# A decoder layer on one core: a second value tile, one staging tile for energies and heads, and all five instruction lists written anew

## The chip, the cores and the metric

The kernel runs on one core of a Trainium2 chip. The metric is the device time of one execution in microseconds (us); lower is better. Engines are called as in the profile: PE (TensorE, matmuls), DVE (VectorE), ACT (ScalarE), POOL (GpSimd), and SP (SyncE), which here issues nearly all DMAs.

## The reference

Four batches of 512 tokens with 512 channels go through one layer of three blocks. Each block adds its result to its input and normalises each row.

```python
Q, K, V = (X @ W.T + b for each of Wq, Wk, Wv)          # 16 heads of 32; Q, K scaled by 32 ** -0.25
scores  = where(causal, Q @ K.T, -inf)
x = layernorm(x + softmax(scores) @ V @ Wo.T + bo)
q, k    = ctx @ Wq.T + bq, ctx @ Wk.T + bk              # 512 x 128, from a context of 256 channels
x = layernorm(x + x @ softmax(q @ k.T).T)               # over the 512 x 512 energies of the batch
xq = quantise(rms_norm(x))                              # 8-bit steps with a scale for each row
x = layernorm(x + ((silu(xq @ sign(Wg).T) * (xq @ sign(Wu).T)) @ sign(Wd).T))    # hidden 2048
```

## The kernel before

A step s is one half batch of 256 tokens (two tiles t of 128); batch b has steps 2b and 2b+1, and a label such as `op1.0.1` means batch 1, half 0, tile 1. For precision most operands are held as two 16-bit parts, a high part that ACT writes and a low part (the rest) that POOL or DVE writes, and PE multiplies high by high, low by high and high by low.

The work of a step, by the names in the lists:

- `lw`, `lg`, `lx`, `lc`, `lr`, `bi`, `sm` (SP): loads of weights, of the 12 pieces of 1 MB whose signs the feed-forward block uses, of x, of the context, of rows, of biases. `ws`, `sg`, `xs`, `cs` split them or take their signs; `kb` (POOL) scales the biases, which the first `qk` on ACT waits for.
- `qk`, `va`: projections on PE; ACT and DVE write both parts of queries and keys (tile `qk`) and of values (tile `v`, with a column of ones, set once by a memset).
- `sk` (SP): three DMAs that copy the parts of one head (of four) of a pair of head groups into the tile `st`, where the score matmuls read them. `mx`: scores for the row maxima, reduced by DVE; `nm`: these maxima transposed; `sh` (SP): two DMAs that put them into `st` as a row, so that `st` (PE) computes scores less the maximum.
- `st`, `sx`, `hi`, `lo`: exponentials on ACT, a causal mask on POOL, high and low parts. `pv` (PE): weights by values; `ov`: division by the row sum.
- `to`: the heads' output is split into the staging tile `ohl` (ACT, POOL) and turned by a transposing DMA (SP) for `op`, the output projection. `os` and `tx` (the same kind of turn, tile `rhl`) lead to `xm`, the cross product.
- `cp`, `en`, `ez`, `ta`: the context's projections, the energies of a batch in four tiles, their softmax, their split into the staging tile `ehl` and their turn by DMA into `aT`, which `xm` reads.
- `n1`, `n2`, `tq`, `ib`, `ga`/`gg`, `uu`, `hw`, `hd`, `hh`, `dn`, `zn`: quantisation and the feed-forward block in 8 units, the last norm and the store.

What sets the order of the work is five lists written into the file, one for each engine (`SP_ORDER`, `PE_ORDER`, `ACT_ORDER`, `DVE_ORDER`, `POOL_ORDER`). Each engine takes its list strictly in order; a step whose inputs are not there holds up all that follows in its list. In PE's list the number behind @ is the PSUM bank (of 8) that the step uses; a bank is opened again when the engine that empties it is done.

`v` holds one batch, so ACT's copy of the first values of a batch waits until the last `pv` of the batch before has read it: `wait(act, pv_done, s // 2 * 2, 0)`. `ohl` has one slot for each tile of a step, `ehl` two slots for the four energy tiles: a slot is written again when the turn that read it has landed.

## Time and profile before

| what | value |
|---|---|
| median of 3 runs (lowest to highest) | 622.56 us (620.17 to 625.86) |
| profiled execution, time / span | 619.0 us / 617.3 us |
| busy in the span: PE, DVE, ACT, POOL | 583.5, 487.6, 413.0, 395.0 us |
| mean granted clock of TensorE | 0.987 |
| DMA: q1, issued by SP | 58.89 MB, 36.4% of 16 engines' span |

The span goes from the first to the last instruction of the profiled execution; its time holds 1.7 us more around it. A busy PE is the union of its matmuls. In the rows further down, a bracket with an arrow says how long an engine was idle before an instruction and what ended that; "SPq" is SP's queue, whose duration is that of issuing, not that of the transfer. L635 issues the stacks, L646 the energies' turns, L600 the sign pieces, L1122 reduces the maxima.

### The profile page before, as it was taken

Reading aid. Unit: us, or ns where it says so; the run is one execution under the profiler, and the core shown is the slowest. Engines: PE = TensorE matmul, PEld = TensorE weight load, DVE = VectorE, ACT = ScalarE, POOL = GpSimd, SP = SyncE. Lnnn points to the kernel's source line nnn. Section 1 sums busy time; section 2 is a strip of 40 time slices with the busy share of each in tenths; the row PEclk is TensorE's granted clock in tenths of the full one; section 3 lists DMA queues with packets and bytes.
Section 4 is the critical chain, followed back from the end, with each engine's and each line's share of the span. In section 5 each row is a group of like instructions: output and inputs, shape, how many; then the busy total and the mean of one; then the engine's idle time right before and its main releaser. Section 6 shows DMA issues by size and latency. Waiting matters only on the chain.

```text
span 617.3 us, 13871 instructions
## 1 busy us (share of the span) xinstructions
PE 583.5 (95%) x5100; PEld 389.1 (63%) x5100; DVE 487.6 (79%) x1296; ACT 413.0 (67%) x773; POOL 395.0 (64%) x518
## 2 busy tenths in 40 slices
...
GB/s 302 323 206 230 253 174 53 129 256 86 10 47 105 91 70 37 49 158 91 78 39 46 146 69 19 3 103 120 36 51 53 105 87 36 10 90 56 19 35 34
DMA packets 90851, 60.29 MB, mean 98 GB/s; under 512 B 65056, under 2 KB 81952, under 8 KB 89248
## 3 DMA queue, kind: packets, MB, share of 16 engines
q1 hardware_dynamic: 90240, 58.89, 36.4%
...
## 4 chain that ended last, share of the span: by engine, by line
PE 66%; SPq 11%; DMA 6%; DVE 6%; ACT 6%; issue 3%; POOL 2%; ACTq 0%; POOLq 0%; DVEq 0%
PE ps_b L700 24%; PE ps_b L851 16%; PE ps_b L866 14%; SPq L635 9%; PE ps_b L795 4%; PE ps_b L774 4%; PE ps_b L757 2%; DMA st<-qk 2%; PE ps_b L753 1%; DMA oT<-ohl 1%; DMA bx<-in_b_x_dram 1%; DVE ps_b L1122 1%; ACT ps_b L961 1%; ACT p L947 1%; ACT ph L884 1%
## 5 line engine op out<-in xcount | busy, mean ns | idle before, releaser
L1122 DVE CUSTOM_DVE_ANT_0 ps_b<-ps_b,future 128x256 f32<-128x256 f32 (+3 forms) x256 | 118.7, 517 | 16.9 <-PE ps_b L757 10.4
L1317 POOL TENSOR_TENSOR ph<-p,ph 128x512 f16<-128x512 f32 x96 | 110.0, 1161 | 27.2 <-ACT ph L884 26.5
L851 PE MATMUL ps_b<-xqT,sg 128*128 128x256 f16 x1024 | 124.9, 272 | 0.1
L866 PE MATMUL ps_b<-sd,hp 128*128 128x512 fp8e4 x512 | 119.1, 379 | 0.0
L1313 POOL TENSOR_TENSOR hp<-gt,hp 128x512 f16<-128x512 f32 x64 | 74.0, 1161 | 56.6 <-ACT hp L884 56.2
L851 PEld LDWEIGHTS ps_b<-xqT,sg 128*128 128x128 fp8e4 x1024 | 98.0, 98 | 19.0 <-ACT p L947 0.6
L700 PE MATMUL ps_b<-xhl,wh 128*128 128x256 f16 x480 | 84.8, 275 | 1.4 <-DVE wl L1073 1.3
L866 PEld LDWEIGHTS ps_b<-sd,hp 128*128 128x128 f16 x512 | 48.6, 98 | 50.0 <-POOL hp L1313 1.5
L1274 POOL TENSOR_SCALAR_AFFINE_SELECT p<-p 128x256 f32<-128x256 f32 (+1 forms) x96 | 46.5, 494 | 46.2 <-ACT p L947 45.7
L700 PE MATMUL ps_b<-xhl,wl 128*128 128x256 f16 x240 | 66.0, 275 | 0.0
L947 ACT ACTIVATE p<-ps_b 128x512 f32<-128x512 f32 x96 | 54.1, 594 | 16.8 <-PE ps_b L774 16.5
L884 ACT ACTIVATE ph<-p 128x512 f16<-128x512 f32 x96 | 58.0, 634 | 9.3 <-POOL p L1274 9.0
L884 ACT ACTIVATE hp<-gt 128x512 f16<-128x512 f32 x64 | 39.9, 628 | 30.8 <-DVE gt L1239 28.1
L1060 DVE TENSOR_TENSOR ph<-ps_b,ph 128x512 f16<-128x512 f32 x64 | 43.2, 685 | 20.9 <-ACT ps_b L961 20.9
L774 PE MATMUL ps_b<-st 128*128 128x256 f16 (+1 forms) x384 | 53.9, 260 | 1.7 <-DVE tops L1122 1.2
L1032 ACT ACTIVATE gt<-gt 128x512 f32<-128x512 f32 x64 | 40.1, 626 | 19.5 <-DVE gt L1226 18.9
L700 PEld LDWEIGHTS ps_b<-xhl,wh 128*128 128x128 f16 x480 | 47.3, 99 | 9.1 <-DVE wl L1073 1.9
L1231 DVE SCALAR_TENSOR_TENSOR gt<-gt,ps_b 128x512 f32<-128x512 f32 x64 | 43.6, 682 | 11.6 <-ACT gt L1032 11.0
L1226 DVE TENSOR_TENSOR gt<-ps_b,invb 128x512 f32<-128x512 f32 x64 | 43.6, 686 | 9.6 <-POOL hp L1313 5.9
L795 PEld LDWEIGHTS ps_b<-v,ph 128*128 128x128 f16 x1376 | 46.4, 97 | 6.4 <-DVE tops L1122 1.2
L795 PE MATMUL ps_b<-v,ph 128*128 128x65 f16 (+2 forms) x1376 | 48.5, 184 | 0.5 <-DVE ph L1060 0.3
L1239 DVE SCALAR_TENSOR_TENSOR gt<-gt,ps_b 128x512 f32<-128x512 f32 x64 | 43.1, 682 | 5.4 <-PE ps_b L851 4.5
...
## 6 DMA issues: line engine op xcount, KB each, us to landing
...
```

Of the source, the lines that this page charges most:

```text
L635: sp.dma_start(st[DH * r:DH * (r + 1), q:k + 1:k - q, j, :, :], qk[DH * j:DH * (j + 1), gp, first:first + step + 1:step, :, :])\
L700: ins = pe.matmul(ps, lhs(hl, c), rhs(hr, c), start=n == 0, stop=n == len(todo) - 1)
L774: ins = pe.matmul(ps[:, col:col + HALF - first], st[:, Q_SLOTS + 2 * gp + kt // 2, j, g % 2, kt % 2 * P:(kt % 2 + 1) * P], st[:, (2 * s + ...
L795: ins = pe.matmul(ps[:, col:col + width], ph[:, n % PH_SLOTS, half, at:at + P], v[:, kt, HG * g + j, first:first + width], start=kt == hal ...
L851: ins = pe.matmul(ps[:, a * HALF:(a + 1) * HALF], sg[:, ("gg", "uu").index(name), c, ht * P:(ht + 1) * P], xqT[:, c, :], start=c == 0, sto ...
L866: ins = pe.matmul(ps[:, :], hp[:, (UNITS * s + n) % HP_SLOTS, h, a, t * P:(t + 1) * P], sd[:, ht, :], start=ht == h == 0, stop=ht == HT - ...
L884: act.activation(out_, in_, ACT.Copy, scale=scale).then_inc(signal, 1)
L947: act.activation(p32[:, m % P32_SLOTS, :], ps[:, :], ACT.Exp, scale=EXP_SCALE).then_inc(p_exp.sem, 1)
L1122: ins = dve.tensor_tensor_reduce(scores, scores, future[:, S - width:S], 1.0, -3e38, ALU.add, ALU.max, tops[:, g // 2, j:j + 1, g % 2, qt ...
L1274: pool.affine_select(out=blocks, in_=blocks, pattern=[[0, len(cols)], [1, P]], compare_op=ALU.is_ge, fill=0.0, base=0, channel_multiplier= ...
L1313: pool.tensor_tensor(slot[:, 1, :, :], tg[:, n % 2, :, :], slot[:, 0, :, :], ALU.subtract)\
L1317: pool.tensor_tensor(out_, in_, hi, ALU.subtract).then_inc(signal, 1)
```

## The change

The value tile has two copies; batch b uses copy b mod 2, and ACT's copy of values waits for the weighing of the batch before the last one. The staging tile `ehl` is gone: energies are split into `ohl`, in the slot t mod 2. So that neither overwrites the other, energies wait until the heads of the batch before are turned, and heads until the energies of their own batch are turned. The scratch for dynamic DMAs falls from 4096 to 1024. All five lists are new: the same steps in another order (about one word in six stands at its old place), and PE's banks are dealt out anew. Of the lists the beginnings of SP's and ACT's are shown; further down the new ACT list has `sg9` and `sg10` right behind `va1.0.0`, where the old one has `sg8` and `sg9` right ahead of it.

```diff
 SP_ORDER = """
-lw0.0 lw0.1 lw0.3 lw0.2 lw2.0 lw1.1 lw1.3 lw2.1 lw1.0 sm lw1.2 lx1 lw2.2 lw3 bi lw2.3 lc0 lg0 lg1 lr0 lr1 sk0.0.0.2
-sk0.0.0.0 sk0.0.0.1 sk0.0.1.3 sk0.0.0.3 sk0.0.1.2 lg2 sk0.0.1.1 lg3 sk0.0.1.0 lx2 lg4 sk0.1.0.0 sh0.0.0 sk0.1.0.2
-sk0.1.0.3 sk0.1.0.1 lg5 lg6 ta0.0 ta0.1 sh0.0.1 lg7 lx3 sk0.1.1.2 sk0.1.1.0 sk0.1.1.1 sh0.1.0 sk0.1.1.3 lg8 ta0.2 lg9
-sh0.1.1 sk1.0.0.1 sk1.0.0.0 sk1.0.0.2 to0.0.0 to0.0.1 sk1.0.0.3 tx0.0.0 lc1 ta0.3 sk1.0.1.0 sk1.0.1.2 tx0.0.1 lg11
+lw1.1 lw1.2 lw0.0 lw1.3 lw0.1 lw1.0 lw2.1 bi lw0.2 lw0.3 lw2.2 lc0 lx1 lw2.0 lw3 lw2.3 sm lg0 lg1 lr1 lr0 sk0.0.0.1
+lg2 sk0.0.0.2 sk0.0.1.3 sk0.0.0.0 sk0.0.0.3 lx2 lg3 sk0.0.1.1 sk0.0.1.0 lg4 ta0.0 sk0.0.1.2 ta0.1 lg5 sk0.1.0.0
+sh0.0.0 sk0.1.0.3 sk0.1.0.1 sk0.1.0.2 lg6 ta0.2 lg7 ta0.3 sh0.0.1 lc1 lg8 sk0.1.1.0 sk0.1.1.1 sk0.1.1.3 sk0.1.1.2
+sh0.1.0 lg9 lx3 lg10 sh0.1.1 to0.0.0 sk1.0.0.1 to0.0.1 sk1.0.0.0 sk1.0.0.3 sk1.0.0.2 tx0.0.0 sk1.0.1.0 tx0.0.1
...
 ACT_ORDER = """
-lx0 xs0.0.0 ws0.0 xs0.0.1 ws0.1 ws0.2 ws0.3 ws1.0 ws1.1 bv ws1.2 ws1.3 ws2.0 ws2.1 ws2.2 wx qk0.0.0 ws2.3 ws3 cs0.0
-qk0.0.1 cs0.1 sg0 qk0.0.2 qk0.0.3 va0.0.0 sg1 cp0.0 cp0.1 va0.0.1 xs0.1.0 xs0.1.1 en0.0 qk0.1.0 sg2 qk0.1.1 ez0.0
-en0.1 nm0.0.0 ta0.0 ez0.1 sg3 en0.2 qk0.1.2 va0.1.0 ez0.2 ta0.1 sg4 st0.0.0.0 qk0.1.3 hi0.0.0.0 st0.0.0.1 va0.1.1
...
-nm0.1.1 to0.0.1 st0.1.1.4 sx0.1.1.3 sx0.1.1.5 sx0.1.1.6 qk1.0.2 st0.1.2.0 st0.1.2.1 ov0.1.0 sx0.1.2.2 hi0.1.1.1
-hi0.1.1.4 en0.3 hi0.1.2.0 ez0.3 st0.1.2.4 st0.1.3.0 qk1.0.3 st0.1.3.1 ov0.1.1 hi0.1.2.1 hi0.1.2.4 sx0.1.2.3 st0.1.3.4
-sx0.1.2.5 sx0.1.2.6 sx0.1.3.2 tx0.0.0 ta0.3 hi0.1.3.0 hi0.1.3.1 sx0.1.3.3 sx0.1.3.5 sx0.1.3.6 hi0.1.3.4 ov0.1.2
-tx0.0.1 sg8 sg9 va1.0.0 ov0.1.3 va1.0.1 to0.1.0 to0.1.1 nm1.0.0 xs1.1.0 xs1.1.1 n10.0.0 n10.0.1 sg10 sg11 ib0
+lx0 xs0.0.0 xs0.0.1 ws0.0 ws0.1 ws0.2 ws0.3 ws1.0 ws1.1 ws1.2 ws1.3 cs0.0 cs0.1 ws2.0 ws2.1 ws2.2 qk0.0.0 ws2.3 ws3 bv
+qk0.0.1 qk0.0.2 sg0 wx qk0.0.3 sg1 va0.0.0 va0.0.1 cp0.0 cp0.1 xs0.1.0 xs0.1.1 sg2 en0.0 en0.1 ez0.0 ez0.1 ta0.0 ta0.1
+qk0.1.0 en0.2 sg3 ez0.2 qk0.1.1 nm0.0.0 sg4 qk0.1.2 en0.3 ta0.2 ez0.3 ta0.3 sg5 va0.1.0 va0.1.1 st0.0.0.0 st0.0.0.1
+hi0.0.0.0 hi0.0.0.1 qk0.1.3 nm0.0.1 st0.0.0.2 st0.0.1.0 st0.0.1.1 hi0.0.0.2 hi0.0.1.0 xs1.0.0 xs1.0.1 sg6 ov0.0.0
...
 POOL_ORDER = """
-k0 k1 kb cs0.0 cs0.1 xs0.1.0 xs0.1.1 rb0.0.0 rb0.0.1 rb0.1.0 rb0.1.1 ta0.0 ta0.1 st0.0.0.0 lo0.0.0.0 st0.0.0.1
+k0 k1 cs0.0 cs0.1 kb xs0.1.0 xs0.1.1 rb0.0.0 rb0.0.1 rb0.1.0 rb0.1.1 ta0.0 ta0.1 ta0.2 ta0.3 st0.0.0.0 st0.0.0.1
...
-        v = sb("v", [P, T, NH, VW], F16)
+        v = sb("v", [P, 2, T, NH, VW], F16)
...
-        ehl = sb("ehl", [P, 2, 2, S], F16)
...
             def turn_energies(b, t):
                 wait(sp, ta_lo, b, t + 1)
                 wait(sp, x2_sum, 2 * b, 0)
-                turn(aT, t, ehl[:, t % 2, :, :], ta_in[t % 2])
+                turn(aT, t, ohl[:, t % 2, :, :], ta_in[t % 2])
...
-                                            v[:, kt, HG * g + j, first:first + width],
+                                            v[:, s // 2 % 2, kt, HG * g + j, first:first + width],
...
             def values(s, t):
-                wait_for(act, vconsts, 1)
+                wait_for(act, vconsts, 2)
                 act.wait_ge(*filled("va", s, t))
                 ps = bank_of("va", s, t)
-                wait(act, pv_done, s // 2 * 2, 0)
-                split(v[:, 2 * (s % 2) + t, :, 0:DH], ps[:, :].rearrange("p (h d) -> p h d", h=NH), v_hi.sem, 1 / WSCALE)
+                wait(act, pv_done, s // 2 * 2 - 2, 0)
+                split(v[:, s // 2 % 2, 2 * (s % 2) + t, :, 0:DH], ps[:, :].rearrange("p (h d) -> p h d", h=NH), v_hi.sem, 1 / WSCALE)
...
             def flip_energies(b, t):
                 wait(act, e_norm, b, t + 1)
                 wait(act, ta_in[t % 2], b, t // 2 * 16)
-                split(ehl[:, t % 2, 0, :], e32[:, t % 2, :], ta_hi.sem)
+                wait(act, to_in[t % 2], 2 * b, 0)
+                split(ohl[:, t % 2, 0, :], e32[:, t % 2, :], ta_hi.sem)
 
             def flip_heads(s, t):
                 wait(act, o_out, s, NG)
                 wait(act, to_in[t], s, 0)
+                wait(act, ta_in[t], s // 2, T // 2 * 16)
                 split(ohl[:, t, 0, :].rearrange("p (g d) -> p g d", g=NG), o[:, s % 2, :, t, :], to_hi.sem)
...
-                dve.memset(v[:, :, :, DH:DH + 1], 1.0).then_inc(vconsts, 1)
+                for i in range(2):
+                    dve.memset(v[:, i, :, :, DH:DH + 1], 1.0).then_inc(vconsts, 1)
...
-    nc = bacc.Bacc("TRN2", target_bir_lowering=False, num_devices=1, dynamic_dma_scratch_size=4096)
+    nc = bacc.Bacc("TRN2", target_bir_lowering=False, num_devices=1, dynamic_dma_scratch_size=1024)
```

## Rows read from the trace of the kernel before

**Rows 1.** The stretches: busy us (x instructions) of PE, PEld, DVE, ACT, POOL; PEclk; DMA; GB/s.

```profile
0.00:26.00 26.00, 14.96 (x102) 10.76 (x103) 13.97 (x24) 15.90 (x28) 16.88 (x17) 1.00 0.90 324
...
58.00:96.00 38.00, 31.17 (x329) 20.42 (x328) 29.04 (x90) 32.98 (x62) 30.28 (x37) 0.82 0.72 198
96.00:132.00 36.00, 33.52 (x369) 21.44 (x367) 26.41 (x82) 31.64 (x61) 22.49 (x32) 1.00 0.61 139
132.00:600.00 468.00, 463.19 (x4047) 312.16 (x4046) 386.57 (x996) 305.76 (x581) 306.33 (x414) 1.00 0.28 68
...
611.40:617.30 5.90, 0.00 (x0) 0.00 (x0) 2.55 (x5) 0.00 (x0) 2.48 (x6) 0.80 0.24 89
```

**Rows 2.** PE's waits, whole span: us in total, times, longest.

```profile
PE ps_b L757 <- DMA st<-qk: 5.3, 5, 2.1
```

**Rows 3.** SP's queue in order of time, 57 to 82 us: start, us, form, xcount.

```profile
57.84 0.58 SPq L600 DMA_DIRECT2D gt<-in_sgT_dram  x1
...
58.97 7.34 SPq L646 DMA_TRANSPOSE aT<-ehl  x2
...
70.71 5.82 SPq L635 DMA_DIRECT2D st<-qk  x9
...
80.47 1.31 SPq L646 DMA_TRANSPOSE aT<-ehl  x1
```

**Rows 4.** DVE in order of time, 74 to 97 us; in brackets the idle time before.

```profile
79.83 0.70 DVE L1122 CUSTOM_DVE_ANT_0 ps_b<-ps_b,future 128x512 f32<-128x512 f32 x1 [5.21 <-PE ps_b L753]
...
85.25 0.43 DVE L1143 TENSOR_TENSOR ps_b<-ps_b,o 128x224 f32<-128x224 f32 x1
...
85.88 0.42 DVE L1148 TENSOR_TENSOR o<-ps_b,osum 128x256 f32<-128x256 f32 x1
...
95.61 0.27 DVE L1129 SCALAR_TENSOR_TENSOR mrow<-ps_b,mrow 16x128 f16<-16x128 f32 x1
```

**Rows 5.** ACT in order of time, 120 to 127 us.

```profile
122.98 0.60 ACT L884 ACTIVATE v<-ps_b 128x512 f16<-128x512 f32 x1
```

**Rows 6.** SP's queue, 340 to 354 us.

```profile
343.89 1.25 SPq L646 DMA_TRANSPOSE aT<-ehl  x1
```

**Rows 7.** DMA issues by form: median us from issue to landing at the end.

```profile
aT<-ehl SPq DMA_TRANSPOSE x16, 3.2
```

**Rows 8.** ACT in order of time, 346 to 352 us.

```profile
349.85 1.14 ACT L884 ACTIVATE ohl<-o 128x512 f16<-128x512 f32 x2
```

**Rows 9.** PE in order of time, 20 to 24 us.

```profile
22.80 0.61 PE L700 MATMUL ps_b<-wh,xhl 128*128 128x512 f16 x2 [3.15 <-DVE wl L1073]
```

**Rows 10.** ACT in order of time, 17 to 22 us.

```profile
20.39 0.84 ACT L926 ACTIVATE qk<-ps_b,bqk 128x256 f16<-128x256 f32 x2 [2.65 <-POOL bx L1375]
```

**Rows 11.** POOL in order of time, 15 to 24 us.

```profile
19.49 0.28 POOL L1374 TENSOR_SCALAR bqk<-bqk 128x8 f32<-128x8 f32 x1 [3.95 <-DMA bx<-in_b_x_dram]
```

**Rows 12.** SP's waits, 26 to 82 us: us in total, times, longest.

```profile
SPq L635 <- DVE qk L1104: 1.5, 1, 1.5
SPq L600 <- ACT sg L911: 1.1, 1, 1.1
```

**Rows 13.** ACT in order of time, 30 to 58 us.

```profile
49.41 1.90 ACT L911 ACTIVATE sg<-gt 128x2048 fp8e4<-128x2048 f32 x1
...
53.84 0.62 ACT L884 ACTIVATE ehl<-e 128x512 f16<-128x512 f32 x1
```

**Rows 14.** SP's queue, 90 to 131 us.

```profile
99.20 5.80 SPq L635 DMA_DIRECT2D st<-qk  x9
105.11 3.34 SPq L646 DMA_TRANSPOSE oT<-ohl  x2
```

**Rows 15.** PE's waits, 96 to 132 us.

```profile
PE ps_b L700 <- DMA oT<-ohl: 1.2, 1, 1.2
```

**Rows 16.** Other stretches, for the granted clock (PEclk).

```profile
79.00:89.30 10.30, 9.32 (x89) 5.83 (x87) 9.22 (x28) 7.46 (x13) 5.63 (x8) 0.50 0.82 249
89.30:96.00 6.70, 5.15 (x80) 3.01 (x79) 6.30 (x19) 6.70 (x15) 5.76 (x7) 1.00 0.02 5
```

More of the change, by code:

```diff
@@ L248 @@
+zn3.0.1 ga3.1.1 hh3.1.0 hh3.1.1 ga3.1.2 ga3.1.3 hh3.1.2 hh3.1.3 ga3.1.4 ga3.1.5 hh3.1.4 hh3.1.5 ga3.1.6 ga3.1.7
+hh3.1.6 hh3.1.7
 """
 DVE_ORDER = """
-k0 xs0.0.0 ws0.0 xs0.0.1 ws0.1 ws0.2 ws0.3 ws1.0 ws1.1 ws1.2 ws1.3 wx ws2.0 ws2.1 ws2.2 bv qk0.0.0 ws2.3 ws3 qk0.0.1
-qk0.0.2 qk0.0.3 va0.0.0 cp0.0 cp0.1 va0.0.1 bo mx0.0.0.0 mx0.0.0.1 en0.0 mx0.0.0.2 mx0.0.1.0 mx0.0.1.1 mx0.0.1.2 en0.1
-en0.2 ez0.0 qk0.1.0 qk0.1.1 ez0.1 nm0.0.0 mx0.0.2.0 mx0.0.2.1 mx0.0.2.2 ez0.2 mx0.0.3.0 mx0.0.3.1 va0.1.0 mx0.0.3.2
```

427 lines of the change are left out of this document (216 added, 211 removed).

## The prediction

> **What bounds the kernel now.** Read the stretches first [rows 1]: what counts is where TensorE (PE) stands idle, since its matmuls are the same before and after. From 132 to 600 us it is busy for 463.19 of 468 us: 4.8 us to win there. The tail after its last matmul is 5.9 us. The rest of the idle time lies in the head: 11.0 us before 26 us (weights arrive), then 6.8 us of the 38 us from 58 to 96, and 2.5 us from 96 to 132. In the head another engine sets the pace. The list of PE's waits [rows 2] shows stacks (st<-qk, the copies that put queries and keys where the score matmuls read them) as a main cause. Their issues stand in SP's queue [rows 3]: from the sign load at 57.84 to the stacks at 70.71 it waits next to nothing, and the first stack of the second pair of head groups goes out only at 70.71. VectorE (DVE) idles 5.21 us for it until 79.83 [rows 4] and then works without a break to 95.88, 16 us, on row maxima that all later steps need. From there ScalarE (ACT) is the busiest after PE, 31.64 of 36 us [rows 1]. So a new order can win in the head, a little in the middle, and nothing in the tail, where the last down products come in the same way.
>
> **The second value tile.** It lets ACT copy the values of batch b before the weighing of batch b-1 has ended. In the shown execution that copy for batch 1 runs at 122.98 with no idle time of ACT ahead of it [rows 5]: the engine was late, not the tile. PE takes its list in order and is 99% busy from there on, so an earlier start only moves work: nothing gained, and the bound is the 4.8 us of idle time after 132 us [rows 1]. The second memset of ones is some 0.1 us on an idle DVE: nothing. The readers of v only address another tile in turn; no operation changes in size. The scratch falls from 4 KB to 1 KB; the DMAs here are issued by SP and ACT, so I count nothing.
>
> **The shared staging tile.** Two waits are new. Energies of batch b wait until the heads of batch b-1 are turned; these lie far apart. Heads of batch b wait until all four energy tiles of that batch are turned. In batch 2 the last of those turns is issued from 343.89 for 1.25 us [rows 6], an energy turn lands 3.2 us after its issue [rows 7], so by about 348.3, and ACT takes the heads at 349.85 [rows 8]. The wait is covered by 1.5 us. If the cover went, the exponentials and tanh steps behind it on ACT would wait as long: 0 to +2 us for a batch, taken as 0. In batch 0 the old order could not stand: it took the heads first and the fourth energy tile later. That is why en0.3, ez0.3 and ta0.3 move far ahead on four engines.
>
> **The start, 0 to 26 us.** Weight chunks of K now come first, those of Q later. By the issue order the first matmul starts some 1.5 us later. But the next hard stop is the value projection at 22.80, which waited 3.15 us for the last V chunk [rows 9]. Its low part stands on DVE behind the first query step, which on ACT stood behind POOL's bias scaling [rows 10, 11]: it waited 2.65 us for it. In the new order POOL scales the bias behind two context steps, so this stop stays near 20.4 us on ACT, although bias and K come sooner. PE has one projection more behind it by then and stalls for the context weights instead. Sum: 0, between -1.5 and +1.5 us.
>
> **The head, 26 to 96 us.** SP is the queue to follow. Ahead of the second pair's stacks of step 1 it issued 12.9 us of other things (two sign loads, two energy turns, a shift row, a sign load, x). The new order puts there again three sign loads, two turns (ta0.2, ta0.3), the shift row and a context load: the same to within 1 us. But lg5, ta0.0 and ta0.1, which stood there, now come still earlier, ahead of the first pair's stacks. A sign load takes 0.58 us, a turn 1.31 us when free (80.47), and both turns together 7.34 us when two loads of 1 MB were ahead of them [rows 3]. So SP gets 3.2 to 7.9 us more to do, less the 1.5 and 1.1 us that it waited there before [rows 12]: +0.6 to +5.3 us. The new list asks for the stacks of head 0 first, which is worth one stack, -1 to -2 us. DVE's 16 us chain takes in one more divide (like that from 85.25 to 86.30, 1.05 us), a transposed row of maxima (0.27) and a query step of two operations (by the one of 0.42, some 0.9): +2.2 us [rows 4]. Sum: +0.8 (0.6 - 2 + 2.2) to +6.5 us (5.3 - 1 + 2.2). A single load stands directly ahead of each turn now, as at 80.47, so I take the lower part: +3.
>
> **The head, 96 to 132 us.** Here the new order gives back. On ACT the list from the second shift row to the first value copy of batch 1 loses two sign pieces at 1.90 us and five smaller ones (en0.3, ez0.3, ta0.3, an exponential, a high part) at about 0.62 [rows 13]: 6.9 us less, since they were done earlier or (one sign piece) are done later. On SP the turn to0.0.0 was issued at 105.11, behind nine stack DMAs of 5.80 us [rows 14], and PE waited 1.2 us for it [rows 15]; it now stands ahead of them. PE can get back no more than its idle time: 2.5 us here and 1.5 us from 89.3 to 96 [rows 1, 16]. Sum: -1 to -5, taken -3.5 as ACT has over 6 us of room.
>
> A rule of the Trainium skill speaks against my counting of the queue. DMA: Bandwidth & Descriptors, section Issuing engines are not separate DMA queues, says that the time in which a sequencer starts DMAs is usually small beside the DMA itself. Here nine stack DMAs keep SP for 5.82 us [rows 3], 0.65 us each, and their order sets when DVE may go on; the trace disagrees. By that rule SP's part (+0.6 to +5.3) would be nothing and the sum some 2 us lower.
>
> **After 132 us.** All lists are new. Counted in steps of PE's list from 132 us on, the new one is as tight as the old: between a transposed maximum and the first score that needs it lie at least 2 steps (before 3), between project_out and its cross at least 7 (before 6). The bound is -3 (of 4.8 us of idle time) to +5 us, taken 0. Tail: 0.
>
> **Sum.** 0 + 3 - 3.5 + 0 = -0.5 us against the profiled execution's 619.0 us (span 617.3): 618.5. The median of the three runs, 622.56, lies 3.6 us above that execution, so I expect 622 us as a median. A measurement of this kernel can tell about 1% (6.2 us) from no change, so this is no change.
>
> **Rivals.** First, slower: SP's queue becomes the bound. Place: ta0.1 and ta0.3, each behind a 1 MB load that has not drained. Price: the pair that took 7.34 us less two free turns of 1.31, so 4.7 us for each of the two [rows 3]; the head is then +3 + 9.4 - 3.5 = +9 and the time 631. It decides from the point where two turns need over 4 us of issue each. For it speaks that four turns now share that queue with seven sign loads; against it the free turn at 80.47. Chance 0.18.
>
> Second, faster: the turns are free, DVE's 5.21 us gap closes because head 0 is asked for first, ACT's relief is paid out in full. Then -1 from 26 to 96, -5 from 96 to 132, -2 later: -8, time 614. For it speaks that DVE idled there; against it that the stacks come no earlier in SP's order. Chance 0.24.
>
> Third, the clock. The granted clock was 0.50 from 79.0 to 89.3, just after PE had stood waiting for stacks, and 1.00 afterwards [rows 16]. It cost little, as DVE was the bound. If a longer stall puts such a stretch where PE is the bound (after 96), it costs half of 10.3 us, +5: 627. Chance 0.05. The Trainium skill, TensorE: Matmul & The Clock Gate, section HAM oscillation — how this bites in real kernels, says that waits on DMAs can put the array back to its slow clock; the row agrees.
>
> That the change does not do what it says (the value tile never in the way) is in the forecast, chance 0.53, whose own range is 616 to 628.
>
> **How the numbers follow.** Faster by over 1% is most of the second rival and a little of the forecast's low end: 0.24. Slower by over 1% is most of the first rival and some of the forecast's and the clock's high ends: 0.18. The rest, 0.58, is no change. The range goes to both rivals: 613 to 631.
>
> **What would show it.** Right: PE idle from 58 to 96 us at 6 to 10 us and from 96 to 132 under 2 us; PE still over 98% busy from 132 to 600; sk0.1.1.0 issued between 70 and 76 us; DVE's chain of maxima ending at 97 to 101; value copies that are ready before the last weighing without PE gaining. Wrong: two energy turns of over 4 us each on SP (slower); that chain ending before 95 (faster); a stretch at half clock after 96; ACT idle for several us ahead of a heads copy, or over 10 us of PE idle after 132, which would be the shared tile or the new lists in the middle.

## The result, and the profile of the changed kernel

The changed kernel took **625.49 us** (median of 17 runs, 623.42 to 629.01), the kernel before in the same rounds 620.33 us (618.63 to 626.59): a ratio of **1.0065 (1.0044 to 1.0086)**, some 4 us slower where half a microsecond less was forecast. Repeated in other rounds it gave 1.0098 (1.0066 to 1.013). So the loss is 4 to 6 us; it is smaller than the 1% bound of the forecast, and larger than its own interval. The profiled execution took 627.9 us (span 626.2), 8.9 us more than that of before; part of this is scatter, since it lies 2.4 us above its median and that of before 1.3 us below its own.

The stretches of the changed kernel, with the columns of [rows 1]:

```profile
0.00:26.00 26.00, 16.88 (x115) 12.33 (x116) 15.14 (x23) 16.25 (x29) 18.10 (x18) 1.00 0.88 324
26.00:58.00 32.00, 24.70 (x160) 15.30 (x158) 18.46 (x67) 21.40 (x35) 9.42 (x8) 0.95 0.97 234
58.00:96.00 38.00, 30.60 (x288) 20.36 (x288) 28.93 (x107) 32.90 (x59) 26.13 (x33) 0.87 0.73 234
96.00:132.00 36.00, 33.14 (x417) 22.45 (x417) 27.85 (x85) 33.81 (x67) 22.62 (x29) 1.00 0.41 90
132.00:600.00 468.00, 458.95 (x4003) 308.70 (x4002) 388.88 (x994) 302.29 (x576) 308.34 (x420) 1.00 0.31 68
...
72.00:82.00 10.00, 7.37 (x43) 5.30 (x43) 4.77 (x17) 7.45 (x12) 6.80 (x10) 0.54 0.91 285
...
364.00:377.00 13.00, 9.67 (x87) 5.19 (x86) 7.89 (x16) 5.27 (x11) 6.32 (x8) 0.87 0.52 81
371.00:376.00 5.00, 4.79 (x18) 2.02 (x19) 1.73 (x5) 0.41 (x2) 1.34 (x2) 0.66 0.28 52
```

Beside [rows 1], PE idles 9.1 instead of 11.0 us in the first 26 us, 7.3 from 26 to 58, 7.4 instead of 6.8 from 58 to 96, 2.9 instead of 2.5 from 96 to 132, and 9.1 instead of 4.8 after that. From 26 to 58 us the kernel before had this row, so 2.6 us of idle time:

```profile
26.00:58.00 32.00, 29.37 (x209) 19.27 (x208) 22.13 (x94) 23.15 (x39) 11.89 (x11) 1.00 0.72 220
```

Two places stand out: 26 to 58 us, and 364 to 377 us, where PE is idle for 3.3 us and a half clock begins. PE's waits over the whole span, beside [rows 2]:

```profile
PE ps_b L757 <- DMA st<-qk: 9.0, 7, 3.8
...
PE ps_b L774 <- DMA st<-mrow: 3.3, 2, 2.6
...
PE ps_b L700 <- DMA x1T<-rhl: 1.9, 1, 1.9
```

Idle time alone misses the half clock. So I use **lost time** below: PE's list holds the same matmuls in every kernel, and each step has a duration when nothing waits and the clock is full (2.59 us for a projection, 0.22 for a score, some 564 for all; an estimate from the steps that nothing held up). The start of a step, less these durations of all steps ahead of it in the list, is the time lost until then. Taken from the profiled execution of each kernel, in stretches of that work (the first 100 us end about where the first scores of batch 1 stand; the third is the stretch around the first cross product of batch 2, `xm2.0.0`):

```
lost us up to ...      100   320   340   end   sum
before                37.0   6.9   0.2   3.2  47.4
changed               41.6   4.9   4.9   4.9  56.3
changed, repeated     41.4   5.6   4.2   4.2  55.4
tiles_old_lists       36.6   8.2   0.2   3.7  48.8
new_head_old_rest     40.2  10.6   0.2   3.4  54.5
old_head_new_rest     37.6   7.5   2.9   3.9  52.0
old_head_new_rest_2   38.2   9.9   4.8   3.9  56.8
signs_after_stacks    42.6   5.1   2.8   4.7  55.2
signs_and_act         41.1   5.3   4.7   4.3  55.4
signs_act_chain       43.8   5.5   4.6   4.6  58.5
early_shift           38.1   5.2   4.5   5.1  53.0
early_shift_signs     40.6   5.1   4.4   4.6  54.7
sg8_back              40.4  13.4   2.7   4.5  61.1
second_shift_early    46.0   5.4   2.8   4.3  58.6
before_stacks_first   42.9   8.9   0.2   3.0  55.0
cross_later           40.0   5.3   6.5   3.7  55.6
rows_early            41.9   5.2   0.7   4.3  52.1
first_shift_rows      42.8   5.2   0.7   4.9  53.6
both_shifts_rows      46.6   4.4   0.7   4.1  55.8
before_rows_late      38.1   8.7   1.7   4.0  52.5
```

The head costs some 4 us more, the cross of batch 2 another 4 to 5, and between them the new lists lose less than the old. One profile stands behind each line, so a difference of a microsecond or two says little: the unedited new head alone lies between 40.0 and 41.9 in five profiles, and its last exponential of batch 0 ends between 120.8 and 123.0 us.

**The head.** SP's queue of the changed kernel from 47 to 85 us, with the columns of [rows 3]:

```profile
47.21 4.69 SPq L635 DMA_DIRECT2D st<-qk  x3
51.95 2.42 SPq L646 DMA_TRANSPOSE aT<-ohl  x1
...
64.70 1.28 SPq L646 DMA_TRANSPOSE aT<-ohl  x1
66.02 0.58 SPq L600 DMA_DIRECT2D gt<-in_sgT_dram  x1
66.64 3.15 SPq L646 DMA_TRANSPOSE aT<-ohl  x1
69.83 1.23 SPq L643 DMA_DIRECT2D st<-mrow  x2
...
73.83 7.83 SPq L635 DMA_DIRECT2D st<-qk  x12
```

The second pair's stacks of step 1 go out at 73.83 (before 70.71, [rows 3]). Ahead of them one head's three DMAs (4.69 us) and the turns of 2.42 and 3.15 us (1.28 when free) were slow behind loads. DVE, and below it PE, show who stood for that:

```profile
82.81 0.70 DVE L1125 CUSTOM_DVE_ANT_0 ps_b<-ps_b,future 128x512 f32<-128x512 f32 x1 [5.93 <-PE ps_b L753]
...
102.53 0.27 DVE L1132 SCALAR_TENSOR_TENSOR mrow<-ps_b,mrow 16x128 f16<-16x128 f32 x1
```

```profile
75.80 2.31 PE L774 MATMUL ps_b<-st 128*128 128x128 f16 x14 [2.63 <-DMA st<-mrow]
```

DVE's gap is as in [rows 4], 3 us later, and the last maxima come 6.9 us later (95.61 to 102.53): from the gap to their end DVE takes 20.0 us instead of 16.05, and idles for 2.9 of them instead of 0.5. PE, which had passed this place without a wait of this kind, stands 2.63 us for a shift row, and from 72 to 82 us its granted clock is 0.54 on average, so at half for nearly the whole stretch. ACT stood longer for sign pieces too; its waits from 26 to 64 us, where the kernel before has one of 0.7:

```profile
ACT sg L911 <- DMA hp<-in_sgT_dram: 6.5, 2, 4.2
ACT sg L911 <- DMA gt<-in_sgT_dram: 3.2, 2, 2.6
```

**Batch 2.** The chain of work that ended last, from 353 to 376 us (start, us, engine, what):

```profile
353.95 4.00 DMA rows<-in_x_dram
...
358.02 2.51 POOL rows L1352 x2
360.52 2.24 POOL xhl L1320 x2
362.76 1.11 POOL ph L1320
363.88 1.11 POOL hp L1316
364.99 1.12 POOL rhl L1320
...
366.13 4.83 DMA x1T<-rhl
...
371.21 4.44 PE ps_b L700 x12
```

Residual rows that SP asks for at 353.95 (`lr4`) land at 358.0. GpSimd works without a break from there, but in order, and the cross product waits at the end for its turned operand (`tx2.0.0`), whose turn takes 4.83 us here and 3.06 in the kernel before. Then its twelve matmuls take 4.44 us, though 2.75 do at full clock (in `rows_early`, below). What stood ahead of that load in SP's queue:

```profile
348.07 2.17 SPq L676 DMA_DIRECT2D out_dram<-rows  x2
350.97 2.62 SPq L646 DMA_TRANSPOSE oT<-ohl  x1
353.95 0.40 SPq L621 DMA_DIRECT2D rows<-in_x_dram  x1
```

`lr4` overwrites the rows that the two stores of batch 1 (L676) read, so it can't go before they have landed; and a turn (`to2.0.0`) stands ahead of it besides. The second store landed at 353.89, just ahead of the load. ACT's part of this, the last norm of these rows (L1006):

```profile
347.24 0.81 ACT L1006 ACTIVATE rows<-rows,shift,rstd 128x512 f32<-128x512 f32 x1
348.53 0.63 ACT L884 ACTIVATE ohl<-o 128x512 f16<-128x512 f32 x1
349.07 0.80 ACT L1006 ACTIVATE rows<-rows,shift,rstd 128x512 f32<-128x512 f32 x1
...
350.93 0.63 ACT L884 ACTIVATE ohl<-o 128x512 f16<-128x512 f32 x1 [0.23 <-DMA aT<-ohl]
```

The second norm (`zn1.0.1`) stands behind the heads' split. In the kernel before both norms come first and `lr4` goes out 3.9 us earlier (350.05); there GpSimd waited 0.31 us for it:

```profile
353.74 2.50 POOL L1349 TENSOR_TENSOR rows<-rows,bo 128x512 f32<-128x512 f32 x2 [0.31 <-DMA rows<-in_x_dram]
```

The stores too were slower from issue to landing: 3.9 us here against 2.4 in the kernel before (DMA issues by form, 343 to 361 us here, 340 to 358 there).

PE's list has changed here too. `xm2.0.0` starts 12.6 us after the output projection of its tile, `op2.0.0` (358.61 to 371.21), 10 steps further on; in the kernel before it was 26.2 us (359.65 to 385.80) and 35 steps. So the rows come later, and the product that needs them comes sooner.

### The profile page after: what moved, and what is told of

It is laid out like the page before. It is cut to its first block, busy times and chain, and to the rows that moved or that the text cites. A ratio compares the mean times of both kernels' runs of the same rounds, so it can differ in the third digit from the quotient of the medians.

```text
span 626.2 us, 13867 instructions
## 1 busy us (share of the span) xinstructions
PE 584.5 (93%) x5100; PEld 390.9 (62%) x5100; DVE 494.8 (79%) x1297; ACT 414.1 (66%) x773; POOL 394.8 (63%) x518
## 3 DMA queue, kind: packets, MB, share of 16 engines
q1 hardware_dynamic: 90240, 58.89, 37.6%
## 4 chain that ended last, share of the span: by engine, by line
PE 56%; SPq 13%; ACT 8%; POOL 7%; DVE 7%; DMA 6%; issue 3%; POOLq 0%; ACTq 0%; DVEq 0%
PE ps_b L700 20%; PE ps_b L851 14%; PE ps_b L866 14%; SPq L635 9%; PE ps_b L774 3%; PE ps_b L795 3%; SPq L646 2%; PE ps_b L757 2%; DMA st<-qk 2%; ACT ph L884 2%; DMA st<-mrow 1%; PE ps_b L753 1%; DMA rows<-in_x_dram 1%; ACT ps_b L961 1%; ACT ph L960 1%
## 5 line engine op out<-in xcount | busy, mean ns | idle before, releaser
L851 PE MATMUL ps_b<-xqT,sg 128*128 128x256 f16 x1024 | 123.1, 272 | 0.4 <-DVE rows L1181 0.4
L700 PE MATMUL ps_b<-xhl,wh 128*128 128x256 f16 x480 | 86.2, 279 | 0.0
L1234 DVE SCALAR_TENSOR_TENSOR gt<-gt,ps_b 128x512 f32<-128x512 f32 x64 | 43.2, 682 | 9.6 <-ACT gt L1034 8.5
L795 PE MATMUL ps_b<-v,ph 128*128 128x65 f16 (+2 forms) x1376 | 47.2, 183 | 2.0 <-DVE ph L1062 1.1
L700 PE MATMUL ps_b<-aT,x1T 128*128 128x512 f16 x192 | 45.5, 390 | 1.9 <-DMA x1T<-rhl 1.9
```

The lines of the kernel that those rows point to most:

```text
L700: ins = pe.matmul(ps, lhs(hl, c), rhs(hr, c), start=n == 0, stop=n == len(todo) - 1)
L795: ins = pe.matmul(ps[:, col:col + width], ph[:, n % PH_SLOTS, half, at:at + P], v[:, s // 2 % 2, kt, HG * g + j, first:first + width], sta ...
L851: ins = pe.matmul(ps[:, a * HALF:(a + 1) * HALF], sg[:, ("gg", "uu").index(name), c, ht * P:(ht + 1) * P], xqT[:, c, :], start=c == 0, sto ...
```

## The experiments

The questions, in order: do the tiles or the lists cost the time; what in the head; what in batch 2. The theories that an expectation sets against each other are named in it; two come back again and again: that a single misplaced step costs the head its time, and against it (D) that an edit of one step only moves the stop to the next tight place. Ratios are against the kernel before on the same chip, with their 95% intervals.

**Tiles or lists.** `tiles_old_lists` has all of the change but the lists; only the fourth energy tile moves ahead, which the shared tile forces.

```diff
 ACT_ORDER = """
-... st0.0.0.0 qk0.1.3 hi0.0.0.0 st0.0.0.1 va0.1.1 nm0.0.1 ... ta0.2 ... hi0.1.1.4 en0.3 hi0.1.2.0 ez0.3 ... tx0.0.0 ta0.3
+... st0.0.0.0 qk0.1.3 en0.3 hi0.0.0.0 st0.0.0.1 va0.1.1 ez0.3 nm0.0.1 ... ta0.2 ta0.3 ... hi0.1.1.4 hi0.1.2.0 ... tx0.0.0
```

> The tiles of the change (value tile held twice, energies staged in the heads' tile, 1 KB of scratch) with the old lists; only en0.3, ez0.3 and ta0.3 are moved ahead of the heads' copies, as the shared tile demands. Theory A (the head's new lists cost, the tiles nothing): 0.998 to 1.002 of the kernel before, some 620 us. Rival B (a wait at the shared tile or the second value tile costs): about 1.006, some 624 us, with ACT idle ahead of a heads copy or of ta0.3. Rival C (the new lists after 132 us cost): as A.

1.0012 (0.9989 to 1.0036): no loss, so rival B is out, and the lost time is near that of before (48.8 and 47.4). ACT's heads copies of batch 2 run with no idle time ahead of them:

```profile
350.76 1.13 ACT L883 ACTIVATE ohl<-o 128x512 f16<-128x512 f32 x2
```

So the lists hold the loss. Two mixtures were to say which half of them, with `changed_again`, the changed kernel itself, in the rounds of one of them.

```diff
-all lists of the changed kernel
+new_head_old_rest: its order for steps that start before 145 us, the order of before for the rest
+old_head_new_rest: the order of before for steps that start before 140 us, its order for the rest
+old_head_new_rest_2: the same, cut so that the same steps lie ahead of the cut on all engines (143 to 148 us)
```

> All five lists of the changed kernel for the steps that it starts in its first 145 us, and the old lists for the rest; the tiles of the change. Theory A (the head's lists: sign loads ahead of the first stacks): 1.005 to 1.009, 624 to 626 us, with TensorE idle some 7 us from 26 to 58. Rival C (the lists after the head): 0.999 to 1.002, 620 to 621 us.

> The mirror of the run before it: the old lists for the steps of the first 140 us (with the three energy steps moved that the shared tile demands), the changed kernel's lists for the rest, the tiles of the change. Theory A: 0.998 to 1.003, 619 to 622 us. Rival C: 1.005 to 1.009, 624 to 626 us, with several us of TensorE idle ahead of the first cross product of batch 2. If head and rest share the loss, each of the two kernels shows some 1.003.

> The changed kernel once more, unaltered, for a second profile. If the 5 us that TensorE lost ahead of the first cross product of batch 2 belong to its lists, they are there again; if they were the chance of one execution, TensorE is idle under 2 us from 300 to 400. Time as before: 1.004 to 1.009.

> As the run with the old lists ahead and the new ones behind, but the seam lies where the two kernels' lists have done the same steps but for a handful (143 us of the old, 148 of the new), so that no bank of PSUM is caught between them; the seam before cost TensorE 2.4 us at 146 us. Theory A (the loss is the head's): 0.999 to 1.003. Rival C (the lists of the rest cost): 1.005 to 1.009 with less than 1 us lost at the seam. Both cost: 1.003 to 1.005.

In this order: 1.0064 (1.0039 to 1.009), 1.0071 (1.0041 to 1.0102), 1.0098 (1.0066 to 1.013) and 1.0113 (1.0077 to 1.0149). Each half alone seems to cost all of it, which can't be added up, and the table says why: the seams cost time that neither kernel has. In `old_head_new_rest_2` PE waits at the seam, and the granted clock is 0.89 from 140 to 150 us:

```profile
PE ps_b L850 <- DVE qk L1106: 2.3, 1, 2.3
```

The mixtures still show two things apart from the seams: with the old head the first 100 us lose 37.6 and 38.2, with the new one 40.2; and the stop at the cross of batch 2 comes with the new rest (2.9, 4.8) and not with the old (0.2).

**The head: signs, ACT, the chain of maxima.** First the sign loads and pieces went behind the stacks and the queries' work; then ACT's further pieces; then DVE's row of maxima was shortened too.

```diff
 SP_ORDER, signs_after_stacks
-... sk0.0.0.1 lg2 sk0.0.0.2 ... sk0.0.0.3 lx2 lg3 sk0.0.1.1 ...
+... sk0.0.0.1 sk0.0.0.2 ... sk0.0.0.3 lg2 lx2 sk0.0.1.1 lg3 ...
 ACT_ORDER
-... xs0.1.1 sg2 en0.0 ... ta0.1 qk0.1.0 en0.2 ...
+... xs0.1.1 en0.0 ... ta0.1 qk0.1.0 sg2 en0.2 ...
 signs_and_act, besides: SP sk0.0.1.2 ahead of lg4; ACT
-... en0.2 sg3 ez0.2 qk0.1.1 nm0.0.0 sg4 qk0.1.2 en0.3 ta0.2 ez0.3 ta0.3
+... en0.2 ez0.2 qk0.1.1 nm0.0.0 sg3 qk0.1.2 en0.3 ta0.2 ez0.3 sg4 ta0.3
 signs_act_chain, besides: nm0.1.0 earlier on PE (ahead of qk1.0.0), DVE and ACT; DVE
-... mx0.1.3.5 lo0.1.0.5 mx0.1.3.6 lo0.1.0.6 mx0.1.3.7
+... mx0.1.3.5 mx0.1.3.6 mx0.1.3.7 lo0.1.0.5 lo0.1.0.6
```

> The changed kernel with one thing put back: on SP the sign load lg2 goes behind five stacks of the first step instead of one and lg3 behind the sixth instead of the fifth; on ACT the sign piece sg2 that waits for lg2 goes behind the first query step of the second half. Theory A: the stacks land some 5 us earlier, ACT no longer stands 4 us at sg2, and 3 to 4 us of the loss come back: 1.000 to 1.002 of the kernel before. Rival C: nothing comes back, 1.006. Rival D (VectorE's row maxima or a later wait absorbs it): the first stacks land earlier, but the last row maximum of the head still ends at 101 to 103 us and the time stays at 1.005 to 1.007.

> On top of the run that put lg2 and lg3 back: the last stack of the first step also goes ahead of lg4 and the first turn, and on ACT the sign pieces sg3 and sg4 go behind the second query step with its shift row (sg3) and behind the fourth energy tile (sg4), so that nothing of the scores waits behind a sign load. Theory A in its second form (stacks behind loads, ACT standing at sign pieces, and a longer row of work on VectorE): the first row of maxima is out at 49 to 51 us instead of 53, the last one at 97 to 98.5 instead of 99.7 (changed kernel 102.8, kernel before 95.9); time 1.003 to 1.006. Rival D (ACT and the stacks of batch 1 set the end of the head anyway): the last maximum comes earlier, the time stays at 1.006 to 1.008.

> The run above, and VectorE's row of maxima made as short as in the kernel before: two low parts (lo0.1.0.5, lo0.1.0.6) behind the last maximum, the shift row nm0.1.0 ahead of the row and not in it (on TensorE too, in another bank). Theory A: the last maximum out at 95.5 to 97 us, the last exponential of the head at 118 to 119.5 (changed kernel 122.5, before 118.2), time 1.000 to 1.003. Rival D: 1.005 to 1.008 whatever the maxima do.

1.0076 (1.0049 to 1.0103), 1.0091 (1.0064 to 1.0117), 1.0156 (1.0121 to 1.0191): no gain, nearest to rival D, and the last is worse than both its theories. The first did what it was made for at one place and gave it back at the next; ACT's sign pieces, whose first wait was one of 4.16 us:

```profile
42.06 1.91 ACT L911 ACTIVATE sg<-hp 128x2048 fp8e4<-128x2048 f32 x1 [0.61 <-DMA hp<-in_sgT_dram]
...
48.67 1.91 ACT L911 ACTIVATE sg<-gt 128x2048 fp8e4<-128x2048 f32 x1 [4.03 <-DMA gt<-in_sgT_dram]
```

**The head: the shift rows.** `nm0.0.0` and its row `sh0.0.0` open the way to the first exponential (63.2 us, before 56.2). In the changed kernel `nm0.0.0` stands behind two scores of the second pair, which need a stack more.

```diff
 early_shift, PE (the same two places on DVE and ACT)
-... qk0.1.1 mx0.0.2.0 mx0.0.3.0 nm0.0.0 ...
+... qk0.1.1 nm0.0.0 mx0.0.2.0 mx0.0.3.0 ...
 SP
-... ta0.1 lg5 sk0.1.0.0 sh0.0.0 ...
+... ta0.1 sh0.0.0 lg5 sk0.1.0.0 ...
 early_shift_signs: both of this and signs_and_act, sh0.0.0 ahead of lg4
 second_shift_early, SP
-... ta0.2 lg7 ta0.3 sh0.0.1 lc1 ...
+... ta0.2 sh0.0.1 lg7 ta0.3 lc1 ...
```

> The same shift row alone in the changed kernel, sign loads and sign pieces left where the change puts them (its DMA goes ahead of lg5). Theory E: shift row out at 51 to 52 instead of 53.5, first exponential at 60 to 62, last one 1 to 2 us ahead of the changed kernel's 122.4; time 1.004 to 1.007. Rival D: no earlier last exponential.

> The run signs_and_act, and the first shift row no longer behind the second pair's maxima: nm0.0.0 goes ahead of mx0.0.2.0 on TensorE and VectorE, its DMA sh0.0.0 ahead of lg4 and both turns on SP. Theory E (new: from the first exponential to the last one of the head, sx0.1.3.6, ACT takes 59 to 62 us in every kernel run so far, whatever stacks, turns or maxima do; what counts is when the first one starts, 56 to 58 us with the old lists, 60.6 to 64.5 with the new): the shift row is out by 48 instead of 53, the first exponential at 57 to 59.5, the last at 117 to 119.5; time 1.001 to 1.004. Rival D (the first exponential comes earlier, but maxima or stacks later in the head take it back): the last exponential stays at 121 to 122.5, time 1.006 to 1.009.

> The changed kernel with one DMA step moved on SP: the second shift row sh0.0.1 goes ahead of the sign load lg7 and the turn ta0.3 that stand ahead of it. Theory H (this stop and the half clock that follows it are the head's loss): the row lands by 71.5 instead of 74.5 us, TensorE loses under 1 us at st0.0.2.2 (2.4 to 3.4 before), the granted clock is not 0.50 over qk1.0.0, the last exponential of the head ends at 118.5 to 120 instead of 121 to 122.4; time 1.002 to 1.005, against 1.0065 to 1.0098 of the changed kernel. Rival D (ACT's list sets the end whatever happens here): the stop goes, the last exponential stays at 121 or later, time 1.006 to 1.010.

1.0084 (1.0062 to 1.0105), 1.0088 (1.0068 to 1.0107), 1.0131 (1.0077 to 1.0185). The first lost 3.4 us less in the head by its profile, the medians don't show it, and `first_shift_rows` below, with the same edit, lost 42.8 there: that one profile was scatter, as far as these two can tell. The third took away the stop at the second shift row; another came at a maximum, and the clock fell there:

```profile
PE ps_b L757 <- DMA st<-qk: 5.7, 1, 5.7
```

**The head: the give-back.** `sg8_back` puts the sign piece back to where the old list had it, behind the exponentials of batch 0.

```diff
 ACT_ORDER
-... st0.0.3.2 hi0.0.3.0 sg8 ov0.0.2 ... va1.0.0 sg9 sg10 va1.0.1 ... xs1.1.1 ov0.1.3 sg11
+... st0.0.3.2 hi0.0.3.0 ov0.0.2 ... va1.0.0 sg8 sg9 va1.0.1 ... xs1.1.1 sg10 ov0.1.3 sg11
 SP_ORDER
-... lg9 lx3 lg10 sh0.1.1 ... sh1.0.0 lx4
+... lg9 lx3 sh0.1.1 ... sh1.0.0 lg10 lx4
```

> The changed kernel with one sign piece of 1.9 us, sg8, back where the old lists have it, behind the last exponential of the head (sg10 and the load lg10 follow it). Theory E: ACT has 1.9 us less to do between first and last exponential, the last one ends at 120 to 121 instead of 122.4, TensorE's stop at mx1.0.3.2 comes 1.5 to 2 us earlier; time 1.003 to 1.006 if the sign piece behind costs nothing there. Rival F (ACT is not the bound of that stretch, maxima or stacks are): the last exponential stays within 0.5 us.

1.0198 (1.0171 to 1.0225), a miss: ACT's last exponential of batch 0 came at 121.0, inside the scatter of the unedited new head, and the move brought a stop of its own. ACT stood 7.3 us for the moved load, the heads were split late, and PE waited for their turn at the output projection:

```profile
PE ps_b L700 <- DMA oT<-ohl: 5.4, 1, 5.4
```

It can't tell what `sg8` cost. Last, the forecast's second rival counted DVE's gap of 5.2 us in the kernel before [rows 4] as something to win. `before_stacks_first` asks for these stacks first, in the kernel before:

```diff
 SP_ORDER
-... lg5 lg6 ta0.0 ta0.1 sh0.0.1 lg7 lx3 sk0.1.1.2 sk0.1.1.0 sk0.1.1.1 sh0.1.0 sk0.1.1.3 lg8 ...
+... lg5 sh0.0.1 lg6 ta0.0 sk0.1.1.2 sk0.1.1.0 sk0.1.1.1 sk0.1.1.3 ta0.1 lg7 lx3 sh0.1.0 lg8 ...
```

> The kernel before, all tiles and lists as they were, but on SP the second shift row goes ahead of the sign load lg6, and the four stacks of the second pair of step 1 ahead of the turn ta0.1, the sign load lg7 and x. If SP's queue sets the head of the kernel before as well (VectorE stood 5.2 us at 79.8 for these stacks): that gap shrinks to under 2 us, the last maximum comes at 92 to 94 instead of 95.9, time 0.994 to 0.998. Rival D (ACT's list sets the end, and lg7 comes late for its sign piece): 0.999 to 1.004.

1.0063 (1.0035 to 1.0091), slower than both theories. The gap closed to 2.0 us, and PE paid for it at the shift row that had been moved back:

```profile
PE ps_b L774 <- DMA st<-mrow: 9.0, 1, 9.0
```

**Batch 2.** `cross_later` leaves the rows late and lets PE take other work first; `rows_early` leaves PE's list alone and brings the rows early, as the lists of before have them; `before_rows_late` does the opposite to the kernel before.

```diff
 cross_later, PE (DVE likewise)
-... xm2.0.0 st2.1.1.0 mx2.1.3.4 mx2.1.3.7 st2.1.1.4 gg1.1.4 mx2.1.3.6 ...
+... st2.1.1.0 mx2.1.3.4 mx2.1.3.7 st2.1.1.4 gg1.1.4 mx2.1.3.6 xm2.0.0 ...
 rows_early, ACT and SP
-... zn1.0.0 hi2.1.0.1 to2.0.0 zn1.0.1 va2.1.0 ...
+... zn1.0.0 zn1.0.1 hi2.1.0.1 to2.0.0 va2.1.0 ...
-... zn1.0.0 zn1.0.1 to2.0.0 lr4 to2.0.1 ...
+... zn1.0.0 zn1.0.1 lr4 to2.0.0 to2.0.1 ...
 before_rows_late, from the kernel before: ACT zn1.0.1 behind to2.0.0; SP
-... zn1.0.0 zn1.0.1 lr4 to2.0.0 to2.0.1 ...
+... zn1.0.0 zn1.0.1 to2.0.0 lr4 to2.0.1 ...
```

> The changed kernel with the first cross product of batch 2, xm2.0.0, behind six other steps of TensorE (four scores and maxima, one gate, one maximum) that stood behind it, and VectorE's sum two steps later. Both profiles of the changed kernel lose 4.2 to 4.9 us there, none of the kernels with the old lists does. If the place is the cause: under 2.5 us lost there, time 1.003 to 1.006. Rival G (the turned rows come late whatever stands ahead, or the loss moves to the next wait): 4 us or more lost between the projections and the second cross product, time 1.006 to 1.009.

> The changed kernel with two steps moved in batch 2: ACT's last norm zn1.0.1 directly behind zn1.0.0, and on SP the load of the residual rows lr4 ahead of the heads' turn to2.0.0, as in the old list. If GpSimd's wait for these rows is the loss in batch 2: rows landed by 356.5 instead of 358, GpSimd's wait under 3 us instead of 4.5, TensorE loses 2.5 us or less around xm2.0.0 instead of 4.2 to 4.9, time 1 to 2 us less than the changed kernel. Rival: the store ahead of the load ends when it did, nothing moves.

> The kernel before with the two steps of batch 2 put where the new lists have them: on ACT the last norm zn1.0.1 behind the heads' copy to2.0.0, on SP the load of the rows lr4 behind the turn to2.0.0. If late rows alone cost it: GpSimd waits 3 us or more for them, TensorE loses 2 us or more between 350 and 380 us that it did not lose before, time 1.004 to 1.008. If it takes the changed kernel's cross product, which stands 6 steps behind the second project_out instead of 23: GpSimd waits as long, TensorE loses under 1 us, 0.999 to 1.002.

`cross_later`: 1.0123 (1.0099 to 1.0147), worse; PE now waited in the work that had been moved up. That is late for the same reason: DVE, in whose list it stands, waits 1.7 us for GpSimd (360 to 385 us):

```profile
PE ps_b L774 <- DVE ph L1062: 2.3, 1, 2.3
PE ps_b L774 <- DVE rows L1181: 1.0, 1, 1.0
```

`rows_early`: **1.0024 (0.9996 to 1.0052)**, more back than its theory gave. GpSimd's wait halves, and the stop and its half clock are gone; POOL, then the stretch, then its DMAs from 365.9 to 370 us (queue: packets, MB, share of 16 engines; then the form and its time to landing):

```profile
357.83 2.50 POOL L1352 TENSOR_TENSOR rows<-rows,bo 128x512 f32<-128x512 f32 x2 [2.27 <-DMA rows<-in_x_dram]
...
364.00:377.00 13.00, 12.69 (x115) 7.39 (x113) 12.15 (x29) 8.07 (x16) 9.40 (x16) 1.00 0.34 81
...
q8 instruction: 1, 0.02, 2.2%
...
x1T<-rhl SPq DMA_TRANSPOSE x1, 3.0
```

PE is busy for 12.69 of 13 us there at a clock of 1.00, where the changed kernel had 9.67 at 0.87. On the clock the rows reach GpSimd only 0.2 us sooner, but against PE's list it is more: the turn is issued 6.1 us after the first output projection (`op2.0.0`) starts, in the changed kernel 7.5. And the turn itself is 1.8 us shorter. In the changed kernel a fetch of instructions (one packet of 16 KB, queue q8 above) starts 2.4 us after the turn's issue, and 79 of the turn's 1024 data packets start behind it. All ten profiles of kernels with the new lists throughout and late rows show this (fetch 1.9 to 2.5 us after the issue, 17 to 454 packets behind it, 4.3 to 4.8 us to landing). In the three with early rows the fetch comes 2.5 to 2.65 us after the issue, at most 9 packets start behind it, all within 0.1 us, and the turn lands in 3.0 to 3.1 us. So it does with the old lists, where the fetch comes 5.2 us after the issue. The margin is thin: in the repeated changed kernel and in `rows_early` the fetch comes at the same 2.5 us, with 17 and 9 packets behind it and landings at 4.6 and 3.0 us.

`before_rows_late`: **1.0069 (1.0045 to 1.0094)**. By its medians, two words moved in the kernel before cost it as much as the whole change. POOL, then one of PE's waits (345 to 400 us), then the stretch, which in the kernel before had PE busy for all of its 35.00 us:

```profile
359.23 2.50 POOL L1349 TENSOR_TENSOR rows<-rows,bo 128x512 f32<-128x512 f32 x2 [4.41 <-DMA rows<-in_x_dram]
...
PE ps_b L851 <- DVE gt L1231: 1.0, 1, 1.0
...
350.00:385.00 35.00, 32.95 (x314) 21.98 (x312) 27.03 (x57) 24.54 (x48) 23.64 (x26) 1.00 0.27 69
```

The cross of this list stands far enough behind, and PE doesn't wait for it. The late rows get at PE by another way: GpSimd is late, DVE waits 3.8 us for it in the gates (350 to 376 us; 0.7 in the kernel before), and PE waits for DVE. That bears out the first theory (2 us or more lost from 350 to 380 us), by a way that it didn't name. Step for step, its profile runs 1.4 us behind that of before already ahead of the moved words, where the lists are the same, so that is scatter; it loses 2.9 us between there and 380 us (the table's stretches divide it), and 0.9 us later, which is not explained.

Two more joined the head's edits to the early rows, since the head might gain once the later stop no longer took what it won.

```diff
 first_shift_rows: early_shift and rows_early
 both_shifts_rows: early_shift, second_shift_early and rows_early
```

> The changed kernel with the early rows of batch 2 (rows_early) and the first shift row early (early_shift), nothing else. If the head's part of the loss is the first shift row standing behind the second pair's maxima: TensorE's lost time by the first score step of batch 1 within 1.5 us of the kernel before, 0.996 to 1.000, the changed lists then beat the old ones. Rival D (the head's stops only move, ACT's list sets the end): as rows_early, 1.001 to 1.004.

> The changed kernel with the first shift row early (as in early_shift), the second one early, and the rows of batch 2 early. Theory H: the last exponential of the head at 117.5 to 119.5, TensorE's lost time at the first score step of batch 1 as in the kernel before (within 1 us), time 1.000 to 1.003. Rival D: 1.006 or more.

1.0023 (1.0003 to 1.0044), the same as `rows_early` alone, and 1.0074 (1.0045 to 1.0103). No version beat the kernel before.

## Why the prediction was wrong

Its time, 622, was 3.5 us short of the median and inside its range, but that is luck: it stood on a median of three runs, 622.56, and that of 17 runs was 620.33. Half a microsecond off that is 619.8, 5.7 us short. Its sign was wrong, and two steps of the sum failed.

**"After 132 us ... the new one is as tight as the old ... taken 0."** This is the one whose cause the runs show: 4.3 us of lost time at one place (4.9 and 4.2 against 0.2 and 0.2 with the old lists), and by the medians 2.5 to 4.6 us (1.0065 and 1.0098 against 1.0024). The step counted two distances in steps of PE's list. It left out the path of the residual rows, norm on ACT, store and load on SP, GpSimd's list, turn, cross. It took the smallest distance of the whole list, which hides that this one fell from 35 steps to 10. And a count of steps is not a time: PE's steps there are scores of 0.22 us as well as projections of 2.59. That the late rows are the cause in the new lists is shown by `rows_early`, where three profiles lose 0.7 us there; `before_rows_late` shows that late rows cost the old lists some 2.9 us too, though in the gates and not at the cross. Whether late rows would cost less with the cross at its old distance in the new lists was not tried. How 1.4 us of lateness makes over 4: 1.4 at the issue of the turn, 1.8 in the turn that runs into the fetch, and 1.7 by the half clock (the cross takes 4.44 us, in `rows_early` 2.75), in all 4.9, of which 4.2 show in the lost time (4.9 against 0.7). That the late rows cause the stop is shown; that the fetch holds the turn's last packets is read from thirteen profiles that agree and was not tried by itself. The forecast's sign for this stretch, PE over 98% busy, held (458.95 of 468 us is 98.1%) and was too coarse to see the loss.

**"The head, 96 to 132 us ... taken -3.5 as ACT has over 6 us of room."** Lost time up to the first scores of batch 1 grew by some 3.5 us (mean 41.0 of the five profiles with the unedited new head, 37.5 of the five with the old one), where start and head together were forecast half a microsecond shorter. Over equal work the start won 2 us, 26 to 96 lost 6.5 and 5.3 us more in the two profiles of the changed kernel (forecast +3, up to +6.5), and 96 to 132 gave nothing back. PE's wait of 1.2 us at the output projection [rows 15] went, as forecast, and others took its place (100 to 140 us):

```profile
PE ps_b L757 <- DMA st<-qk: 2.4, 3, 1.3
PE ps_b L795 <- DVE ph L1062: 1.1, 2, 0.9
```

The bound of -5 had also been more than the 4.0 us of idle time that the step itself names. The count of ACT's list was right: from the second shift row (94.9 us before, 101.8 after) to the first value copy it shortened from 28.1 to 22.4 us. But only 2.6 of these 5.7 us lay ahead of the last exponential (it ends at 118.2 and 122.5), since some of the pieces that left the list had stood behind it. That exponential is what the next stacks wait for (SP issues them at 118.24 and 122.52), and PE waits for those, 1.3 us at the longest. And the stretch began 6.9 us later, as the maxima that feed the second shift row ended 6.9 us later: less 2.6, the exponential came 4.3 us late, though ACT idled only 0.7 us on the way (before 0.2). Room on an engine is paid out only ahead of its last needed operation.

**The head, 26 to 96 us**: the chain that the step named did get longer, and the size came at the upper end of its bounds. The stacks went out within the forecast's 70 to 76 us, at 73.83, 3.1 us later than before; the maxima ended at 102.8, not at 97 to 101, since DVE's part grew by 3.9 us (forecast +2.2), 2.4 of them new idle time. But PE loses its time earlier than the step says: over equal work 7 to 8 us more than before from 26 to 58 us, and 1 to 2 us less from 58 to 96. So that this chain is what the head costs is not shown. The first rival's place was right and its price too high: the two turns took 2.42 and 3.15 us, not over 4, 3.0 us more than free ones together; the three stack DMAs of 4.69 us, some 2.7 more than three at 0.65, it had not named. Which edit of the head costs what **stays open**: seven kernels with edits of the new head were tried and two more with the early rows; stops moved, and none gained by its medians.

**The start, 0**: it won 1.9 us of idle time, just outside its bound of 1.5. **The second value tile, 0; the shared staging tile, 0; scratch, 0; tail, 0**: right, together 1.0012. The value copy of batch 1 ran at 124.19, ready some 7 us before the last weighing of batch 0, with no gain. The new wait for the turns was met for 0.23 us in batch 2, so the cover of 1.5 us had gone, at next to no price. (The forecast had added 3.2 us to the end of the turn's issue, while [rows 7] counts from its start; that turn took 4.55 us from its start, so it landed at 348.44, as counted, by luck.) **The third rival**, a half clock where PE is the bound, came true in batch 2 and not behind the head, at 1.7 us and not 5. The Trainium skill, TensorE: Matmul & The Clock Gate, section HAM oscillation — how this bites in real kernels, has the array fall back to its slow clock on waits for DMAs; the rows agree, 0.54 around the wait of 2.63 us for a shift row, and 0.66 from 371 to 376 us behind a wait of 1.9 us that ended with a DMA.

The sum, new lists against old: +3.5 in the head, -2.7 from there to 320 us of work (means 5.2 of four new and 7.9 of three old, without mixtures and edits of the head), +4.3 at the cross of batch 2, +1.1 behind it: +6.2 by the profiles, against +4.0 and +6.1 by the two measurements. With early rows (+0.5 at the cross) it is +2.4 by the same terms, and +1.5 (-0.2 to +3.2) measured.
